# Attention and MXFP8-style FFN on one core: probabilities turned by a diagonal of inverse sums, row statistics moved to VectorE, and a new hand-written order

## What is computed

```python
# x (4, 512, 512), ctx_1024 (4, 512, 256), Wq, Wk (128, 256), gate_w, up_w (2048, 512), down_w (512, 2048)
query = jnp.einsum('bnc,dc->bnd', teacher_features, Wq) + bq
key = jnp.einsum('bnc,dc->bnd', teacher_features, Wk) + bk
energy = jnp.einsum('bnd,bmd->bnm', query, key)
attention = jax.nn.softmax(energy, axis=-1)
x_m = jnp.einsum('bln,bmn->blm', teacher_logits, attention)
...
def _mx_dequant(t):
    blocks = t.reshape(rows, feat // _BLOCK, _BLOCK)          # blocks of 32
    scales = jnp.maximum(jnp.max(jnp.abs(blocks), axis=-1) / _FP8_MAX, _EPS)
    q = (blocks / scales[..., None]).astype(jnp.float8_e4m3fn).astype(jnp.float32)
    return (q * scales[..., None]).reshape(rows, feat)
def _mx_linear(x2d, w):
    return _mx_dequant(x2d) @ _mx_dequant(w).T
...
h = jax.nn.silu(_mx_linear(x2d, gate_w)) * _mx_linear(x2d, up_w)
out = _mx_linear(h, down_w)
...
x = x + xattn(_layernorm(x, axis=-1), ctx_1024, ...)
x = x + ffn(_layernorm(x, axis=-1), ...)
```

## Time and profile before

| what | value |
|---|---|
| runs | 630.29, 1291.2, 630.39 us |
| median | 630.39 us |
| profiled execution | 629.73 us, of which its span is 627.9 us |
| mean granted TensorE clock | 0.988 |
| PE busy | 598.2 us, 95% of the span |
| DVE busy | 491.6 us, 78% |
| ACT busy | 317.0 us, 50% |
| POOL busy | 56.7 us, 9% |

### The profile page before, as it was taken

One profiled execution on the slowest core, in us unless ns is written; L12 is line 12 of the kernel. 1 busy time (PEld: TensorE's weight loads), 2 busy tenths in 40 slices (PEclk: granted clock), 3 DMA queues, 4 the chain that ended last, 5 costly groups with the idle time before them and its releaser, 6 DMA issues.

```text
span 627.9 us, 6981 instructions
## 1 busy us (share of the span) xinstructions
PE 598.2 (95%) x2560; PEld 271.3 (43%) x2560; DVE 491.6 (78%) x439; ACT 317.0 (50%) x463; POOL 56.7 (9%) x70
## 2 busy tenths in 40 slices
PE   4689897999999999999999999999999999999996
PEld 1244343444344444444444444444444444444442
DVE  5978799799889898999899997899987898222110
ACT  2999987765464554555455414625422222333311
POOL 1210210010101000200101003000000000010101
PEclk9899898999999999999999999999999999999999
DMA  8946959997898958587867205729220002777862
GB/s 347 401 108 178 279 147 236 231 229 174 185 228 209 226 125 202 142 160 164 155 135 150 68 1 103 132 67 154 48 34 2 0 1 38 131 128 124 129 122 34
DMA packets 147441, 89.91 MB, mean 143 GB/s; under 512 B 134224, under 2 KB 134352, under 8 KB 142672
## 3 DMA queue, kind: packets, MB, share of 16 engines
q1 hardware_dynamic: 142080, 63.25, 43.1%
q0 software_dynamic: 5328, 26.22, 18.9%
HBM read 25.49 MB, written 8.39 MB: 54 GB/s over the span
## 4 chain that ended last, share of the span: by engine, by line
PE 41%; issue 33%; DMA 10%; ACT 9%; DVE 2%; SPq 2%; POOL 2%; POOLq 0%; ACTq 0%; DVEq 0%
PE bank L685 30%; PE bank L699 7%; PE bank L670 3%; DMA W<-hT 3%; DMA gu_lo<-hT 3%; DMA gu_hi<-hT 2%; POOL out_y L554 1%; ACT h L896 1%; ACT hT L875 1%; ACT h L887 1%; DMA hT<-W 1%; ACT dn L907 1%; DMA gu_hi<-in_ctxT 1%; ACT hT L869 1%; SPq L357 1%
## 5 line engine op out<-in xcount | busy, mean ns | idle before, releaser
L685 PE MATMUL bank<-gu_hi,xT 128*128 128x512 f16 x1024 | 305.6, 379 | 1.5 <-DMA gu_lo<-hT 1.5
L685 PE MATMUL bank<-gu_lo,xT 128*128 128x512 f16 x512 | 194.0, 379 | 0.0
L699 PE MATMUL bank<-dn,hT 128*128 128x512 f16 x768 | 166.6, 379 | 0.0
L685 PEld LDWEIGHTS bank<-gu_hi,xT 128*128 128x128 f16 x1024 | 100.2, 98 | 123.0 <-issue 2.6
L699 PEld LDWEIGHTS bank<-dn,hT 128*128 128x128 f16 x768 | 75.1, 98 | 90.6
L980 ACT ACTIVATE silu<-bank,unscale 128x512 f32<-128x512 f32 x64 | 43.0, 679 | 93.3 <-PE bank L685 52.1
L685 PEld LDWEIGHTS bank<-gu_lo,xT 128*128 128x128 f16 x512 | 50.1, 98 | 60.3 <-issue 0.3
L1497 DVE SCALAR_TENSOR_TENSOR W<-h,W 128x2048 f16<-128x2048 f32 x10 | 22.9, 2292 | 54.1 <-DMA hT<-W 49.2
L670 PE MATMUL bank<-dn,h 128*128 128x512 f32 x128 | 59.8, 626 | 3.5 <-ACT dn L919 3.5
L1465 DVE SCALAR_TENSOR_TENSOR h<-bank,unscale,silu 128x512 f32<-128x512 f32 x64 | 46.5, 746 | 13.6 <-PE bank L685 9.3
L1006 ACT ACTIVATE W<-h 128x2048 f16<-128x2048 f32 x16 | 30.6, 1910 | 47.1 <-DMA hT<-W 26.8
(11 more groups left out here) (92 smaller groups left out, 500.9 us busy)
## 6 DMA issues: line engine op xcount, KB each, us to landing
W<-in_units SPq DMA_DIRECT2D x12, 1024.0 KB, 6.2
W<-hT POOLq DMA_DIRECT2D x12, 1024.0 KB, 6.0
h<-W POOLq DMA_DIRECT2D x6, 1024.0 KB, 6.0
h<-in_xcols SPq DMA_DIRECT2D x4, 1024.0 KB, 14.1
out_y<-y POOLq DMA_DIRECT2D x16, 256.0 KB, 5.1
gu_hi<-in_ctxT SPq DMA_DIRECT2D x4, 512.0 KB, 8.6
h<-in_xrows SPq DMA_DIRECT2D x2, 1024.0 KB, 11.8
out_y<-h SPq DMA_DIRECT2D x2, 1024.0 KB, 6.3
```

The lines of the kernel that those rows point to most:

```text
L685: last = pe.matmul(bank[:, :], xT[:, b % 2, part, k, :], w[:, c, g, j * 512:(j + 1) * 512], start=(m == 0), stop=(m == 3 * HT - 1))
L699: last = pe.matmul(bank[:, :], hT[:, r % 2, a, k, :], dn[:, w, k, :], start=(m == 0), stop=(m == 3 * IT - 1))
```

## The change

Every engine's order is new, and so are `products`, `rounds` and `bank_uses`. Beside that:

- `divide` and PE's transpose of probabilities are gone. `weigh` on DVE multiplies the identity by the inverse sums, which gives a diagonal of 128x128 for each tile of probabilities (in unused columns of `h`). `turn_probs` multiplies the unnormalized probabilities with that diagonal in four ordinary f32 matmuls of 128 columns.
- The sums of the rows after attention come from the accumulator output of `add_attended`; `attended_means` turns them into means. `center` on DVE subtracts the mean from the rows of each batch. The block scales and the rounding are taken from centered, not normalized rows, and the inverse deviation is multiplied into the block scales in `rows_dequant`. ACT keeps one pass with squares (`attended_variances`), for all four batches.
- The last 128 rows (`down(15)`) are read back early (`load_last`), ACT adds the constant (`add_constant`), DVE adds the down product (`add_last`), and SP stores them plainly (`store_last`) instead of `take_down(15)` and `add_out(15)`.
- ACT loads its exponential table with a small activation at the start.
- The waits that kept `hidden_rest` apart from transposing DMAs are gone: on POOL for hidden tiles 1, 2, 3 and 5, on SP for 1, 2 and 5; two new waits on POOL stand ahead of `rows_rest(2)` and `rows_rest(3)`.

```diff
-    products = [(0, 0), (3, 0), (0, 1), (3, 1), (2, 0), (2, 1), (1, 0), (1, 1), (0, 2), (2, 2), (1, 2), (3, 2),
-                (5, 0), (5, 1), (4, 0), (3, 3), (4, 1), (4, 2), (2, 3), (4, 3), (0, 3), (6, 0), (6, 1), (6, 2),
...
+    products = [(2, 0), (0, 0), (0, 1), (2, 1), (3, 0), (3, 1), (1, 0), (1, 1), (5, 0), (4, 0), (4, 1), (4, 2),
+                (1, 2), (6, 0), (6, 1), (5, 1), (2, 2), (0, 2), (4, 3), (0, 3), (6, 2), (6, 3), (1, 3), (3, 2),
...
+        diagonal = [[h[:, nt, 512 + n * P:512 + (n + 1) * P] for nt in range(LT)] for n in range(2)]
...
+            def load_last():
+                sp.wait_ge(x1_stored[B - 1], 16)
+                sp.wait_ge(*rows_lo_done(B - 1))
+                sp.dma_start(last_x, out_rows[RT - 1]).then_inc(last_in, 16)
+
+            def store_last():
+                sp.wait_ge(last_in, 16)
+                sp.wait_ge(last_summed, HT)
+                sp.dma_start(out_rows[RT - 1], last_out).then_inc(last_stored, 16)
...
-            pool.wait_ge(nT_in[0], 48)
+            second_norm(2)
+            hidden_rest(1)
+            pool.wait_ge(hT_in[1], 32)
             rows_rest(2)
-            pool.wait_ge(nT_in[1], 48)
-            hidden_rest(1)
             add_out(0)
-            pool.wait_ge(hT_in[1], 32)
+            add_out(1)
+            second_norm(3)
             hidden_rest(2)
-            pool.wait_ge(hT_in[1], 48)
             hidden_rest(3)
-            add_out(1)
             pool.wait_ge(hT_in[1], 64)
+            rows_rest(3)
             hidden_rest(4)
             add_out(2)
-            second_norm(3)
-            pool.wait_ge(hT_in[0], 80)
             hidden_rest(5)
             add_out(3)
-            pool.wait_ge(hT_in[1], 96)
...
             def turn_probs(b, nt):
+
                 bank = take_bank(f"t{b}.{nt}")
-                pe.wait_ge(probs_ready, LT * b + nt + 1)
-                turn4(bank, [probs[b % 2][:, nt, j * P:(j + 1) * P] for j in range(HT)]).then_inc(probs_turned, 1)
+                pe.wait_ge(diagonal_ready, LT * b + nt + 1)
+                for j in range(HT):
+                    last = pe.matmul(bank[:, j * P:(j + 1) * P], probs[b % 2][:, nt, j * P:(j + 1) * P],
+                                     diagonal[b % 2][nt], start=(j == 0), stop=(j == HT - 1))
+                last.then_inc(probs_turned, 1)
 
...
-            def divide(b, nt):
-                act.wait_ge(rsum_ready, b + 1)
-                nc.scalar.activation(probs[b % 2][:, nt, :], probs[b % 2][:, nt, :], ACT.Copy,
-                                     scale=rsum[:, LT * b + nt:LT * b + nt + 1]).then_inc(probs_ready, 1)
-
...
-            def attended_stats(b):
-
-                act.wait_ge(x1_ready, LT * (b + 1))
-                if b == 1:
-                    act.wait_ge(*rows_lo_done(0))
-                for lt in range(LT):
-                    cols = slice(lt * H, (lt + 1) * H)
-                    last = nc.scalar.activation(early_xw[:, cols], X[b][:, cols], ACT.Copy,
-                                                accum_out=ysum[:, LT * b + lt:LT * b + lt + 1])
-                act.wait_ge(act_step, own.done(last))
-                act.wait_ge(act_step, own.done(
-                    nc.scalar.activation(nmean[:, of(b)], ysum[:, of(b)], ACT.Copy, scale=-1.0 / H)))
+            def attended_variances(b):
+
+                act.wait_ge(ymean_ready, b + 1)
+                if b == 2:
+                    act.wait_ge(*unit_lo_done(U_ALL - 1))
+                elif b > 0:
+                    act.wait_ge(nT_in[0], 16 * b)
+                    act.wait_ge(nT_in[1], 16 * b)
+                if b >= 2:
+                    act.wait_ge(xnorm_ready, b + 1)
+                squares = xparts_of(b).rearrange("p a n -> p (a n)").bitcast(F32)
                 for lt in range(LT):
                     cols = slice(lt * H, (lt + 1) * H)
                     row = slice(LT * b + lt, LT * b + lt + 1)
-                    last = nc.scalar.activation(early_xw[:, cols], X[b][:, cols], ACT.Square,
-                                                bias=nmean[:, row], accum_out=yssq[:, row])
+                    if b < 2:
+                        last = nc.scalar.activation(squares[:, cols], X[b][:, cols], ACT.Square, bias=nmean[:, row],
+                                                    accum_out=ysum[:, row])
+                    else:
+                        last = nc.scalar.activation(squares[:, cols], late_xw[:, cols], ACT.Square,
+                                                    accum_out=ysum[:, row])
                 act.wait_ge(act_step, own.done(last))
-                nc.scalar.activation(var[:, of(b)], yssq[:, of(b)], ACT.Copy, scale=X_SCALE ** -2 / H,
+                nc.scalar.activation(var[:, of(b)], ysum[:, of(b)], ACT.Copy, scale=X_SCALE ** -2 / H,
                                      bias=LN_EPS * X_SCALE ** -2).then_inc(var_ready[b], 1)
-
-            def normalize(b):
-                act.wait_ge(rstd_ready, b + 1)
-                if b == 1:
-                    act.wait_ge(*rows_lo_done(0))
-                src = X[b] if b < 2 else late_xw
-                for lt in range(LT):
-                    cols = slice(lt * H, (lt + 1) * H)
-                    row = slice(LT * b + lt, LT * b + lt + 1)
-                    last = nc.scalar.activation(xw_of(b)[:, cols], src[:, cols], ACT.Identity,
-                                                scale=rstd[:, row], bias=nmr[:, row])
-                last.then_inc(xnorm_ready, 1)
...
+            act.wait_ge(pool_step, 1)
+            nc.scalar.activation(late[:, 1840:1844], mhalf[:, :], ACT.Exp)
...
+            def weigh(b, nt):
+
+                dve.wait_ge(rsum_ready, b + 1)
+                if b >= 2:
+                    dve.wait_ge(probs_turned, LT * (b - 1))
+                dve.tensor_scalar(diagonal[b % 2][nt], idf, rsum[:, LT * b + nt:LT * b + nt + 1], None, ALU.mult
+                                  ).then_inc(diagonal_ready, 1)
+
             def add_attended(b, lt):
 
                 dve.wait_ge(x_in[b], 16)
                 dve.wait_ge(xrstd_ready, b + 1)
                 dve.wait_ge(attended, LT * b + lt + 1)
                 rows = X[b][:, lt * H:(lt + 1) * H]
-                dve.scalar_tensor_tensor(rows, bank_of(f"a{b}.{lt}")[:, :], xrstd[:, LT * b + lt:LT * b + lt + 1], rows,
-                                         ALU.mult, ALU.add).then_inc(x1_ready, 1)
-
-            def attended_stats(b):
-
-                rows = X[b]
-                if b < 2:
-                    dve.wait_ge(x1_ready, LT * (b + 1))
-                else:
+                row = slice(LT * b + lt, LT * b + lt + 1)
+                dve.scalar_tensor_tensor(rows, bank_of(f"a{b}.{lt}")[:, :], xrstd[:, row], rows, ALU.mult, ALU.add,
+                                         accum_out=ysum[:, row]).then_inc(x1_ready, 1)
+
+            def attended_means(b):
+                dve.wait_ge(x1_ready, LT * (b + 1))
+                dve.tensor_scalar(nmean[:, of(b)], ysum[:, of(b)], -1.0 / H, None, ALU.mult).then_inc(ymean_ready, 1)
+
+            def center(b):
+                dve.wait_ge(ymean_ready, b + 1)
+                if b == 1:
+                    dve.wait_ge(*rows_lo_done(0))
+                elif b >= 2:
                     dve.wait_ge(x_in[b], 32)
-                    rows = late_xw
+                src = X[b] if b < 2 else late_xw
                 for lt in range(LT):
-                    last = dve.bn_stats(stats[:, lt, :], rows[:, lt * H:(lt + 1) * H])
-                then(last)
-                for lt in range(LT):
-                    last = dve.bn_aggr(mv[:, lt, :], stats[:, lt, :])
-                then(last)
-                dve.tensor_scalar(nmean[:, of(b)], mv[:, :, 0], -1.0, None, ALU.mult)
-                dve.tensor_scalar(var[:, of(b)], mv[:, :, 1], LN_EPS, X_SCALE ** -2, ALU.add, ALU.mult
-                                  ).then_inc(var_ready[b], 1)
+                    cols = slice(lt * H, (lt + 1) * H)
+                    last = dve.tensor_scalar(xw_of(b)[:, cols], src[:, cols], nmean[:, LT * b + lt:LT * b + lt + 1], None,
+                                             ALU.add)
+                last.then_inc(xnorm_ready, 1)
 
             def rows_scale(b):
                 xw, s = xw_of(b), xscale[:, :]
@@ -1380,9 +1367,11 @@
                 if b > 0:
                     dve.wait_ge(nd_ready, b)
                 then(dve.tensor_reduce(s, blocks(xw), AX.X, ALU.max, apply_absolute_value=True))
-                then(dve.tensor_scalar(s, s, 1.0 / FP8_MAX, TINY * X_SCALE, ALU.mult, ALU.max))
+                then(dve.tensor_scalar(s, s, 1.0 / FP8_MAX, TINY, ALU.mult, ALU.max))
                 invert(s)
                 scalings.append((nv_ready, b + 1))
+                if b >= 2:
+                    dve.wait_ge(var_ready[b], 1)
                 dve.tensor_tensor(blocks(xw), blocks(xw), each_block(rscale[:, :]), ALU.mult).then_inc(nv_ready, 1)
...
+                dve.wait_ge(rstd_ready, b + 1)
```

(12 more changed lines are left out.)

792 lines of the change are left out of this document (400 added, 392 removed), and 8 rows, old and new, of the table products.

## The result

The changed kernel took 640.39 us (median of 4 runs, 639.31 to 640.87), the kernel before 630.91 beside it: a ratio of 1.0151, 95% interval 1.0131 to 1.0172. It is 1.5% slower, where 628 and a range of 617 to 640 had been predicted. Run again later, the same kernel gave 1.0144 (1.0122 to 1.0165). The profiled execution took 640.53 us, with a span of 638.7.

A forecast was written before the change was run, and what follows sets the result against it. PE, busy 95% of the span, bounds the kernel. Last attended row 130.4, 62 products 321.8, downs 165.8, late units 3 and tail 5.0 make a span of 626.0, with profiling offsets 628 us; range 617 to 640.

The forecast's parts named there:

- Part 3: Order up to the first attended product: DVE's queue decides, row sums at 38.2, product at about 46, 3 us later.
- later stages: Behind the late units: DVE has room, moved downs cost nothing, and the dropped turns of hidden_rest are put at zero.
- The last sentence of the prediction: Sign of a wrong prediction: hidden rows' transposes become late because hidden_rest now overlaps them; no size given.
- Part 5: Next units after the attended stage: product (5, 0) 1 us late, units 4 and 5 2 us late, unit 7 hidden.
- Part 1: Diagonals replace divide: an ordinary 128-column f32 product costs 0.24 us a block, 11.5 us instead of 5.8 for 48 blocks.
- rival B: Turning probabilities: the 128-column f32 product costs 0.48 us (or 0.43), 11.5 us more on PE, 636 to 640; 14%.
- Part 2: Moved statistics: center 2.6 us a batch, the sum in add_attended free; DVE about 10 us more, ACT 21 us less.
- Part 4: First to last attended row: PE work 82.9 us plus 1.5 us wait at product (2, 0), ending at 130.4; gain 2.7.
- Rival C: Batch 1's rows arrive late for product (5, 0); landing at 185, PE stands 23 us, 651 in all; 7%.
- Part 6: Tail with a plain store: 5.0 us instead of 5.70, 0.7 saved, bounds 0 and 2.5.
- late units: Term of 3 us in the sum, for PE's waits at the 9th and 12th products.

The follow-up runs named there:

- s3: Changed kernel with batch 0's row sums and diagonals earlier on DVE, and its probability copies ahead of unit 2's magnitude and unit_lo(0) on ACT: 1.0062.
- t1: Changed kernel with the dropped turn-taking waits for hidden tiles 1, 2, 3 and 5 put back on SP and POOL: 1.0084.
- t2: Changed kernel with only SP's wait for the landing of hidden_rest(1) put back: 1.0097.
- b5: Kernel before with only the turn-taking waits around hidden_rest dropped: 1.0000.
- b4: Kernel before with diagonals, last rows stored plainly and ACT's table loaded ahead, all orders and turns as before: 0.9950.
- c2: s3 with t1's waits put back and, on ACT, attended_variances(2) ahead of hidden_lo(0) and rows_magnitude(2) ahead of hidden_hi(1): 1.0031.
- c5: c2 with batch 2's rows ahead of hidden row tile 1, a mistaken bank table, and batch 1's last two diagonals earlier on DVE: 1.0171.
- c6: c2 with batch 2's rows ahead of hidden row tile 1 on every engine and PSUM banks going round by last use: 1.0027.
- s1: Changed kernel with POOL's all-reduce of unit 2's maximum ahead of batch 0's power: 1.0103.
- n1: Changed kernel without POOL's wait for turn_hidden_lo(1) ahead of rows_rest(2) and SP's wait for rows_rest(2) ahead of turn_rows_hi(2): 1.0100.
- c1: s3 with n1's two waits taken out and the same two ACT moves as c2: 1.0039.

## Why the prediction was wrong

**The step that failed: Part 3, "the order on DVE decides".** I added up DVE's instructions to the row sums (38.2) and took every input as ready. One was not. Unit 2's maximum came from POOL at 35.76, and I had costed POOL at nothing: DVE waited 5.20 us in front of `unit_power(2)`, and the sums came at 43.76. The kernel before showed the same gap, 5.86 us ahead of its all-reduce at 37.76, and I had not read POOL's timeline. I had also put 43.2 for the last bank on ACT by adding durations, where `unit_magnitude(2)` waited 3.60 us for DVE's rounding, to 43.88. The forecast of 46 came out at 55.20. With the orders on DVE and ACT changed so that neither wait stands ahead, it came out at 46.13 (s3). So PE's own work in the sum was about right, and what failed was the assumption that every input is there. That s3 meets 46 so closely is in part luck, since its orders are not the ones that I added up. The clock took 2.7 us of the 9.2, which the forecast had not priced either.

**The second step that failed: "later stages", where the dropped turns are put at zero.** They cost 3 to 4 us (t1, t2). I had argued from the kernel before, where `hT` is never late, and missed that the new order takes that slack away (b5 shows 1.0000 with the slack). The last sentence of the prediction names this very risk; it had no price and no chance.

**The rest of 285 to 345**, row 8's wait of 3.65 us, was not seen at all. Part 5 walked batch 1's rows to their product and never batch 2's.

**What held.** Part 1: 16 blocks in 3.73 us, 0.233 a block against 0.24; rival B is false. The Trainium skill's TensorE: Matmul & The Clock Gate (Terms) has transpose mode four times faster for FP32, and the rows show a factor of two (0.233 against 0.12). Part 2: a batch's `center` took 1.67 us, not 2.6. The Trainium skill's VectorE: DVE Perf Modes (The perf-mode tier table) points that way, though half of 2.6 would be 1.3. The sum in `add_attended` adds a read of 0.08 us, without lengthening the pace of 0.67. Part 4: 82.5 us from first to last attended row, against 82.9 and a wait of 1.5; the wait at product (2, 0) was 0.19. The second profile of the same kernel has 84.1 and 1.80, so the 1.9 us gained here are within what two profiles differ by. Rival C is false: product (5, 0), the 9th, did not wait. Part 5: the 12th product, (4, 2), waited 1.59 us for 2. The 9th, which was to wait 1 us, did not, and the 3rd, (0, 1), which I had not listed, waited 0.72; so 2.3 for 3 is near in part by luck. Part 6: the tail was 3.80 us, not 5.0. The 1.9 us saved (2.1 counted from the end of PE's last matmul) are nearer its bound of 2.5 than the 0.7 taken.

**The sum again**, in span: 626.0 predicted, +9.2 start, -1.9 in Part 4, -0.7 late units, -1.2 tail, +5.2 idle between 285 and 345 and +1.7 of lower clock there give 638.3, against 638.7. The 1.7 is the difference between two profiles: from row 8's first product to PE's last matmul are 312.65 us in the changed kernel, with a granted clock of 0.96 from 310 to 350, and 310.97 us in s3, with 1.00.

**What stays open.** With start and turns mended, the changed orders still give 1.003, against 0.995 for b4. The profiles of c2 and b4 differ by 5.5 us of span, and 3.1 of it is there at the first attended product, which starts at 45.25 in c2 and at 42.15 in b4. No experiment here took that away. The forecast had it, as 3 us. Behind it, c2 waits 3.1 us around batch 1's diagonals and 3.3 at row 8, while b4 has waits of its own elsewhere. Moving c2's waits (c5, c6) gave about the same amount back in other places. That these orders ask more of DVE and of the transfers than fits at these two places is my reading, and not shown.

## What to carry to other kernels

When an order is changed, walk every input of each moved instruction back to its engine, the quiet one first: the place of one POOL instruction of 0.38 us was worth some 3 us (s1). A wait that looks idle in the kernel before (turn taking) may hold only because of slack there, so price it where the new order puts it. And run the parts of a change in the old order: here the three that were run so were worth 3 us that the new order hid.

## What the runs showed of the hardware

- When POOL goes from an all-reduce to a power or back, it stands still for at least 5.8 us behind its previous instruction, with nothing shown (5.86 above, 7.87 in s1, up to 8.33 in c2). If it has been idle for that long anyway, nothing comes on top (8.27 and 9.57 above), but for the first change of the program. Between two all-reduces or two powers there is no gap, also with a DMA issue between them (0.35 us idle in s1, at 40.08).
- An accumulating transfer of 1024 KB takes 5.9 us where turns keep the transpositions away and 8.1 to 8.2 beside them; the transpositions of hidden rows lengthen from 4.4 to 5.7.
- An f32 product of 128x128 by 128 columns takes 0.233 us at the full clock, the transpose of the same block 0.12.
- The lower clock behind row 8's wait cost 1.7 us (312.65 against 310.97). The length of that wait did not decide it: the granted clock from 310 to 350 was 0.96 behind waits of 2.65 (t2), 2.83 (t1), 3.31 (c2) and 3.65 us, and 1.00 behind 1.99 (n1), 2.27 (c1) and 3.16 (s3).
